# A fused recommender tower on one core: a split wait, a new cycle order and one more looked-up group

## The reference

```python
e = jnp.stack([tbl_0[ids[:, 0]], ..., tbl_39[ids[:, 39]]], axis=1)      # 2048 x 40 x 32
vi = e[:, _I_IDX, :]; vj = e[:, _J_IDX, :]                               # 780 pairs
z = jnp.einsum('bke,kef,bkf->bk', vi, W, vj)
h = jnp.concatenate([z, dense_ctx], axis=1)                              # 796 columns
h = jnp.maximum(h @ W_top1 + b_top1, 0.0)                                # 512
h = jnp.maximum(h @ W_top2 + b_top2, 0.0)                                # 256
y = h @ W_top3                                                           # 1
```

## Time and profile before

| | before |
|---|---|
| median of three runs | 696.76 us |
| profiled execution: time, span | 699.06 us, 697.2 us |
| TensorE matmul busy | 644.0 us (92%), 4800 records |
| VectorE busy | 580.5 us (83%), 578 instructions |
| ScalarE busy | 70.1 us (10%) |
| GpSimd busy | 460.5 us (66%) |
| L543 multiply, 440 instructions | 495.1 us |
| L567 transform | 242.4 us busy, 33.4 us idle ahead of it |
| L589 reduce | 217.7 us busy |
| L616 look-up | 65.2 us + 7.6 us busy |
| L493 units, 88 | 67.4 us |

### The profile page before, as it was taken

The page is one execution under the profiler, slowest core; times in us unless marked ns, Lnnn a source line. Parts: engine busy times, 40 slices in busy tenths (PEclk is TensorE's granted clock), DMA queues, the critical chain, the costliest instruction groups (busy, mean ns, idle before and its releaser), DMA issues.

```text
span 697.2 us, 11003 instructions
## 1 busy us (share of the span) xinstructions
PE 644.0 (92%) x4800; PEld 187.3 (27%) x4800; DVE 580.5 (83%) x578; ACT 70.1 (10%) x87; POOL 460.5 (66%) x471
## 2 busy tenths in 40 slices
PE   3898988988999999999999999998999999999898
PEld 1232222222223322322222222222222222222143
DVE  6988999999978799889877889889888888888800
ACT  5502001000100100110000000100000000000002
POOL 6777777777777777777777777777777777500000
PEclk9999999999999999999999999999999999999999
DMA  8735202000000110200000200000101000000000
GB/s 322 276 98 194 69 13 74 14 13 14 13 14 15 32 58 13 74 14 13 15 13 15 76 14 14 13 14 14 16 14 15 14 14 13 12 1 1 1 0 1
DMA packets 18944, 28.28 MB, mean 41 GB/s; under 512 B 8448, under 2 KB 16016, under 8 KB 17232
## 3 DMA queue, kind: packets, MB, share of 16 engines
q0 software_dynamic: 14848, 7.63, 7.4%
q1 hardware_dynamic: 3296, 17.57, 6.5%
q10 hardware_dynamic: 752, 2.37, 0.9%
HBM read 27.53 MB, written 0.01 MB: 40 GB/s over the span
## 4 chain that ended last, share of the span: by engine, by line
PE 61%; DVE 34%; issue 3%; DMA 1%; ACT 1%; ACTq 0%; SPq 0%; DVEq 0%
DVE prods L543 26%; PE tps L567 25%; PE zps L589 15%; PE mlp_ps L636 15%; DVE hot L493 6%; PE tps L636 4%; PE mlp_ps L616 2%; DMA ids<-in_hot_ids 1%; DVE eT L500 1%; PE zps L576 1%; DVE parts L482 0%; DVE zs L482 0%; ACTq L467 0%; ACT ids L409 0%; DVE w1s L482 0%
## 5 line engine op out<-in xcount | busy, mean ns | idle before, releaser
L543 DVE TENSOR_TENSOR prods<-tps,eT 128x1024 f32<-128x1024 f32 (+1 forms) x440 | 495.1, 1168 | 72.5 <-PE tps L567 68.8
L371 POOL DMA_INDIRECT rows<-in_table,idx x464 | 459.9, 991 | 144.4 <-issue 141.2
L567 PE MATMUL tps<-eT,weights 32*128 32x512 f32 x1680 | 242.4, 641 | 33.4 <-DVE prods L543 31.1
L589 PE MATMUL zps<-prods,select 128*32 128x512 f32 x1680 | 217.7, 605 | 2.3 <-DVE prods L543 1.5
L567 PEld LDWEIGHTS tps<-eT,weights 32*128 32x128 f32 x1680 | 66.7, 183 | 185.3 <-DVE prods L543 146.4
L636 PE MATMUL mlp_ps<-zs,w1s 128*128 128x512 f32 x182 | 89.8, 615 | 0.0
L589 PEld LDWEIGHTS zps<-prods,select 128*32 128x32 f32 x1680 | 38.2, 108 | 159.4 <-DVE prods L543 98.7
L616 PE MATMUL mlp_ps<-hot,parts 128*32 128x512 bf16 x960 | 65.2, 389 | 14.7 <-DVE hot L493 10.9
L493 DVE TENSOR_SCALAR hot<-ids,code 128x2048 bf16<-128x2048 int16 (+1 forms) x88 | 67.4, 787 | 1.9 <-ACT ids L409 1.6
L387 ACT ACTIVATE zs<-zps 128x512 f32<-128x512 f32 x28 | 16.7, 598 | 326.3 <-PE zps L589 326.3
L636 PEld LDWEIGHTS mlp_ps<-zs,w1s 128*128 128x128 f32 x182 | 31.3, 189 | 55.1 <-issue 55.1
(11 more groups left out here) (31 smaller groups left out, 50.4 us busy)
## 6 DMA issues: line engine op xcount, KB each, us to landing
ids<-in_hot_ids SPq DMA_DIRECT2D x10, 1024.0 KB
rows<-in_table,idx POOLq DMA_INDIRECT x464, 2.4
zs<-in_hot_table SPq DMA_DIRECT2D x4, 512.0 KB, 7.5
w1s<-in_w ACTq DMA_DIRECT2D x1, 1792.0 KB, 7.6
weights<-in_wt SPq DMA_DIRECT2D x1, 1088.0 KB
zs<-in_hot_ids SPq DMA_DIRECT2D x1, 1024.0 KB
weights<-in_wt SPq DMA_DIRECT2D x1, 960.0 KB, 9.1
weights<-in_wt SPq DMA_DIRECT2D x1, 704.0 KB, 7.2
```

What stands on the lines that cost most here:

```text
L371: pool.indirect_dma_start(rows[:, k % ROW_SLOTS, m * EMB:(m + 1) * EMB], None, table, bass.IndirectOffsetOnAxis(ap=idx[:, g, t, m:m + 1], ...
L543: last = dve.tensor_tensor(prods[:, at % PROD_SLOTS, r:to + 1, :], tps[:, pair, r % 2:to % 2 + 1, :], eT[:, (t * GROUPS + c) % ET_SLOTS, : ...
L567: last = pe.matmul(tps[:, (2 * at + half) % PAIR_BANKS, r % 2, :], weights[part, n, :], eT[part, slot, :], start=True, stop=True)
L589: last = pe.matmul(zps[EMB * r:EMB * (r + 1), :], select[:, off:off + EMB], prods[:, at % PROD_SLOTS, r, :], start=kt < KT - 1 and n == fi ...
```

## The change

The changed kernel has the following edits.

- Transform waits ahead of each half, for 2 * at - 2 and for 2 * at - 1.
- Cycles are listed in CYCLES: quad 0 of each chunk is a cycle of one quad, and then come 26 cycles of two, all from an odd n. The `between` order is gone. A cycle with one step now has the order T, R, M, T, R; a cycle with two or more keeps T, M, M, T, R, R.
- HOT_COUNT is (4, 4, 2, 2): group 3 of chunk 1 is looked up, not gathered. It comes first of chunk 1's hot groups, since its table stands in w1s. ET_SLOTS goes from 13 to 14. The 32 units of chunk 1 are spread over chunk 0 as the 24 were, and the loads of the perceptron's weights come after the drain of the new group.
- Units are made 4 quads ahead in every chunk (in the earliest cycles, from quad 4 on, where that is less). The conversions of ids move with them.
- In chunk 3, the 17 batches stand in its first 17 cycles of two. Six steps of the tail, those of the first output tile of layer one for k = 0 to 5, stand alone in cycles n = 37, 39, 41, 43, 45 and 51, and leave the tail.
- ScalarE writes a small tile minus_code and VectorE a tile ones. ScalarE's own way of making units is there, but `by_scalar` is always false: nothing reads these two tiles.

```diff
-ROW_SLOTS, ET_SLOTS, PROD_SLOTS = 6, 13, 3
+ROW_SLOTS, ET_SLOTS, PROD_SLOTS = 6, 14, 3
-HOT_COUNT = (4, 3, 2, 2)
-HOTS = [(t, g) for t in range(CHUNKS) for g in range(HOT_COUNT[t])]
+HOT_COUNT = (4, 4, 2, 2)
+HOTS = [(t, g) for t in range(CHUNKS) for g in ((3, 0, 1, 2) if t == 1 else range(HOT_COUNT[t]))]
+CYCLES = [at for t in range(CHUNKS) for at in [(t * QUADS,)] + [(t * QUADS + n, t * QUADS + n + 1) for n in range(1, QUADS, 2)]]
...
-        for k, block in enumerate(blocks):
-            at = cycles[k if hots else k * len(cycles) // len(blocks)]
+        for at, block in zip(twos, blocks):
...
+    for k, n in enumerate(EARLY_AT):
+        sides[(CHUNKS - 1) * QUADS + n].append(("mlp", CHUNKS - 1, 0, 0, k))
...
+EARLY_AT = (37, 39, 41, 43, 45, 51)
+EARLY = [("mlp", CHUNKS - 1, 0, 0, k) for k in range(len(EARLY_AT))]
+def by_scalar(h, u):
+    return False
-MADE_AHEAD = (2, 4, 4, 4)
+MADE_AHEAD = 4
-            MAKES[side_at - MADE_AHEAD[side_at // QUADS]].append(item[1:])
+            MAKES[max(side_at - MADE_AHEAD, min(side_at, 4))].append(item[1:])
-    return steps, int(len(steps) > 0 and at % QUADS % PER_KT == 0)
...
+            act.wait_ge(code_built, 1)
+            act.activation(minus_code[:, :], code[:, :], ACT.Copy, scale=-1.0).then_inc(codes_turned, 1)
...
-                        if step[0] == HOT_COUNT[0] - 1:
+                        if HOTS[step[0]] == (1, HOT_GROUPS - 1):
...
-                wait(pe, multiplied, 2 * at - 1)
                 for half in range(2):
+                    wait(pe, multiplied, 2 * at + half - PAIR_BANKS + 1)
                     for r in (2 * half, 2 * half + 1):
...
-            for at in range(0, TOTAL, 2):
-                steps, between = steps_of(at)
+            for cycle in CYCLES:
+                at = cycle[0]
+                steps = steps_of(at)
...
+                together = len(steps) > 1
                 transform(at)
-                for _, t, layer, m, k in steps[:len(steps) - between]:
+                if not together and at > 0:
+                    reduce(at - 1)
+                for _, t, layer, m, k in steps:
                     mlp(t, between_banks, layer, m, k)
-                if not steps and at > 0:
-                    reduce(at - 1)
                 look_ups(at)
-                transform(at + 1)
-                if steps:
-                    reduce(at - 1)
-                for _, t, layer, m, k in steps[len(steps) - between:]:
-                    mlp(t, between_banks, layer, m, k)
-                reduce(at)
-                look_ups(at + 1)
+                if len(cycle) == 2:
+                    transform(at + 1)
+                if together:
+                    reduce(at - 1)
+                if len(cycle) == 2:
+                    reduce(at)
+                    look_ups(at + 1)
...
-                        mlp(CHUNKS - 1, last_banks, layer, m, k)
+                        if ("mlp", CHUNKS - 1, layer, m, k) not in EARLY:
+                            mlp(CHUNKS - 1, last_banks, layer, m, k)
```

More of the change, by code:

```diff
@@ L143, in plan_sides @@
         hots = [h for h, (t_, _) in enumerate(HOTS) if t_ == t + 1]
-        cycles = [at for at in range(0, TOTAL, 2) if t * QUADS <= at < (t + 1) * QUADS]
+        twos = [cycle[0] for cycle in CYCLES if len(cycle) == 2 and cycle[0] // QUADS == t]
         first = 3 * M1
@@ L170 @@
         if item[0] == "hot" and item[1] >= HOT_COUNT[0]:
[L171 removed]
+            MAKES[max(side_at - MADE_AHEAD, min(side_at, 4))].append(item[1:])
 def steps_of(at):
[L177 to L178 removed]
+    return [item for item in SIDES[at] if item[0] == "mlp"]
 def use_of(item):
@@ L189 @@
 FIRST_MADE = {unit[0]: at for at, made in MAKES.items() for unit in made if unit[1] == 0}
-SHORTENED_AT = {max(at // 2 * 2 - 4, 4): h for h, at in FIRST_MADE.items() if h >= HOT_COUNT[0]}
-assert len(SHORTENED_AT) == len(HOTS) - HOT_COUNT[0]
+SHORTENED_AT = {max(at - (at % QUADS + 1) % 2 - 4, 3): h for h, at in FIRST_MADE.items() if h >= HOT_COUNT[0]}
+assert len(SHORTENED_AT) == len(HOTS) - HOT_COUNT[0] and set(SHORTENED_AT) <= {cycle[0] for cycle in CYCLES}
 def wait(engine, semaphore, count):
@@ L199, in hots_until @@
 def hots_until(t, g):
-    return sum(h <= (t, g) for h in HOTS)
+    return HOTS.index((t, g)) + 1
 def gathered_until(t, g):
@@ L243, in build @@
         code = sb("code", [PART, UNITS], I32)
+        minus_code = sb("minus_code", [PART, UNITS])
+        ones = sb("ones", [PART, 1])
         hot = sb("hot", [PART, HOT_SLOTS, Q, CHUNK], BF16)
@@ L342, in _ @@
             sp.wait_ge(ids_short, 1)
[L343 removed]
+            sp.wait_ge(hot_made_dve, 2)
             load_ids(2)
@@ L417, in round_part, with make_unit @@
                 act.activation(part_of[g][part], raw_parts[g], ACT.Copy).then_inc(rounded, 1)
+            def make_unit(h, u):
+                if u == [by_scalar(h, u_) for u_ in range(UNITS)].index(True):
+                    act.wait_ge(ids_short, h + 1)
+                act.wait_ge(hot_used, h * UNITS + u - HOT_SLOTS + 1)
+                columns = hot[:, (h * UNITS + u) % HOT_SLOTS].rearrange("p q c -> p (q c)")
+                act.activation(columns, ids16[:, h % 2].rearrange("p q c -> p (q c)"), ACT.Abs,
+                               bias=minus_code[:, u:u + 1]).then_inc(distances, 1)
+                act.wait_ge(distances, made_until(h, u, True))
+                act.activation(columns, columns, ACT.Relu, scale=-1.0, bias=ones[:, 0:1]).then_inc(hot_made_act, 1)
             def drain_hot(h):
@@ L447, in _ @@
             round_part(3, 1)
+            act.wait_ge(code_built, 1)
+            act.activation(minus_code[:, :], code[:, :], ACT.Copy, scale=-1.0).then_inc(codes_turned, 1)
+            act.wait_ge(codes_turned, 1)
+            act.wait_ge(consts_built, 2 + Q)
             shorten(3)
-            for at in range(0, TOTAL, 2):
+            for cycle in CYCLES:
+                at = cycle[0]
                 if at in SHORTENED_AT:
                     shorten(SHORTENED_AT[at])
-                if at == QUADS // 2 * 2:
+                if at == QUADS:
                     act.wait_ge(mlp_loaded, 16 * 5)
-                steps, between = steps_of(at)
-                if not between:
-                    drain_tiles(steps)
+                drain_tiles(steps_of(at))
                 drain_sums(at - 1)
-                if between:
-                    drain_tiles(steps)
-                drain_sums(at)
-                for kind, *step in SIDES[at] + SIDES[at + 1]:
+                if len(cycle) == 2:
+                    drain_sums(at)
+                for kind, *step in [item for quad in cycle for item in SIDES[quad]]:
                     if kind == "hot" and step[1] == UNITS - 1:
                         drain_hot(step[0])
-                        if step[0] == HOT_COUNT[0] - 1:
+                        if HOTS[step[0]] == (1, HOT_GROUPS - 1):
                             for dst, src in ((w1s, w1), (w2s, w2), (w3s, w3), (b1s, b1), (b2s, b2)):
                                 act.dma_start(dst[:], src).then_inc(mlp_loaded, 16)
+                for unit in [unit for quad in cycle for unit in MAKES[quad]]:
+                    if by_scalar(*unit):
+                        make_unit(*unit)
             drain_z(CHUNKS - 1, KT - 1)
@@ L489, in make_unit @@
                     dve.wait_ge(code_built, 1)
-                elif u == (2 if h == 0 else 0):
+                elif u == (2 if h == 0 else [by_scalar(h, u_) for u_ in range(UNITS)].index(False)):
                     dve.wait_ge(ids_short, h + 1)
@@ L511, in _ @@
                            1.0).then_inc(consts_built, 1)
+            dve.memset(ones[:, :], 1.0).then_inc(consts_built, 1)
             rest(0, 0)
@@ L549, in _ @@
                 for unit in MAKES[at]:
-                    make_unit(*unit)
+                    if not by_scalar(*unit):
+                        make_unit(*unit)
                 if at == 0:
```

28 lines of the change are left out of this document (18 added, 10 removed).

## The result

The changed kernel takes 694.12 us in the median of six runs (692.44 to 695.22), the kernel before 698.20 us in the median of its six (696.74 to 700.43). The ratio is 0.9936, with a 95% interval from 0.9920 to 0.9951: faster by 0.6%. The forecast was 690.2 us with a range of 685 to 698. All ratios leave out executions that took over 1.5% longer than the fastest of the same kernel.

The account below looks back on a forecast made before the run. VectorE bounds chunk 0, TensorE chunks 1, 2 and the tail, chunk 3 is mixed. Terms +1.5 - 0.4 - 4.7 + 2.2 - 5.2 = -6.6 us take 696.76 to 690.2 us, range 685 to 698.

Parts of the forecast that it names:

- the tail: After the last reduction, TensorE alone: six steps leave at 0.86 us each, -5.2 us.
- the cycle order of chunk 2: Chunk 2: five cycles with a step between two reductions take the plain order, saving 3.9 of the chunk's 4.7 us.
- the split wait: Transforms on TensorE: first half starts earlier, closing 16 VectorE gaps in chunk 0, -3.0 us; 0.37 per cycle without steps.
- the new group: Chunk 0: eight more units on VectorE cost +5.3 us, look-ups at the chunk's end +0.8; saved gathers give nothing.
- The conversion: Chunk 0, ScalarE: ids converted ahead of the last drain, so VectorE no longer waits 1.61 us, -1.6 us.
- Chunk 1: Second chunk: only the one cycle without work gains, -0.4 us.
- Chunk 3: Last chunk: early steps +3.2, two empty cycles -0.7, dense rows moved to an empty cycle -0.3; together +2.2 us.
- The last cycle: Last of six single-step cycles in the last chunk: the transform of quad 52 comes 0.4 us later.
- the loop of a lone step: Last chunk: cycles T R M T R take 5.47 us against 4.91, five times 0.56, 2.8 us more.
- that the split gives nothing: Rival: both halves' records leave together and gaps stay; sum -1.7, 695.1 us; 0.17 together with a dearer group in chunk 0.
- the slower case: Rival: a transform's second half queues behind the first, ready 0.39 us later in 49 loops, +19 us, 709 us; chance 0.08.
- The better case: Rival: less TensorE idle time at chunk 0's start, 1 to 3 us, and cheaper early steps, 2: 686 us; chance 0.13.

Follow-up runs that it names:

- e3b: Changed kernel with HOT_COUNT (4, 3, 2, 2) as before, so group 3 of chunk 1 is gathered, 29 gathered groups: 685.64 us, 0.9817 of the kernel before.
- e5: Changed kernel without split wait, new looked-up group and early steps, leaving cycle order, earlier units and earlier conversion: 692.25 us, 0.9919 of the kernel before.
- e1b: Changed kernel with the one wait of before ahead of each transform: 697.33 us, 0.9983 of the kernel before.
- e9: Kernel before with one number changed, so ScalarE converts the first ids of chunk 1 ahead of chunk 0's last drain: 695.34 us, 0.9967 of before.
- e4b: Changed kernel with EARLY_AT empty, all steps of the last chunk's perceptron in the tail: 693.37 us, 0.9926 of the kernel before.
- e2b: Kernel before with only the wait split by half: 690.12 us, 0.9885 of the kernel before.
- e1: Changed kernel with one wait per transform, first run, on a chip that stopped engines: 1.0007 of the kernel before (0.9963 to 1.0052).
- e4: Changed kernel with no early steps, first run, on a chip that stopped engines: 0.9954 of the kernel before (0.9912 to 0.9995).

## Why the prediction was right, and where it was off

The forecast said faster, by 6.6 us, mostly from the tail, the cycle order of chunk 2 and the split wait, with the new group as the price. All four have the sign that it gave, and the experiments bear it out: without the wait the kernel is slower, without the group it is faster. Leaving the early steps out made the kernel 0.6 us faster in the profiles: what the tail gained, chunk 3 paid. By its steps:

- **The split wait, chunk 0, -3.0.** Right in mechanism and near in size: 3.65 us for e3b against e5, both without the new group and at full clock. Beside the group's units it is only about 1.4 (e1b), because they fill places where gaps stood. A met wait costs nothing, as assumed: cycles with two steps still take 5.91 us.
- **The new group, +5.3 and +0.8.** Mis-sized. It is 7.2 us in the profiles. The units are 6.3, of which 1.0 is the slow ones, and ScalarE's order at quad 39 costs 0.9, a wait that the prediction did not look for. The 0.8 for the end of the chunk is there, but not from the group: the gap at quad 50 is 1.6 us in the changed kernel, and e3b without the group has 0.7 and 0.8 at quads 49 and 50. It goes with the 0.9 us that e5 is behind e9.
- **The conversion, -1.6.** Right: VectorE's wait is gone, and 1.65 us with it at full clock (e9).
- **Chunk 1, -0.4; chunk 2, -4.7.** Measured -0.6 and -3.9. The five odd cycles, read as 3.9 from the earlier trace rows, gave 3.6 (e5); but the split wait gave chunk 2 only 0.3, not 0.7. A cycle without steps fell from 5.06 to 4.58 us, and the two-step cycle behind a chunk's first quad rose from 5.90 to 6.11: part of what VectorE gains is only time for which TensorE would have waited later.
- **Chunk 3, +2.2.** Measured +3.3. Two steps failed in size. The last cycle was to grow by 0.4 us and grew by 1.05 (7.28 against 6.23 in e4b). And the loop of a lone step is 5.6 us and not 5.47, 0.7 over the five cycles. A reduction with a step behind it takes 617.48 - 616.48 = 1.00, and a lone step 618.53 - 617.48 = 1.05, where the prediction took halves of pairs, 0.92 and 0.96. The page TensorEngine Tiling (Array Packing) of the Trainium skill, Key Properties, says that a change of tiling mode drains TensorE. The trace fits that: a pair shares the price of going in and out, a lone block pays it alone, here 0.08 and 0.09 us more. That it is the drain which costs this, no run here shows.
- **The tail, -5.2.** Measured 5.15.

In the profiled executions the span fell by 6.1 us, from 697.2 to 691.1, close to the 6.6, and that closeness is luck. In the medians the time fell by 4.1. The step that failed here is the one that carried the sum over: that the difference is the same on the profiled execution and on the median. The profile of before had two stretches at half clock in chunk 0, and that of the changed kernel none. The two places in both, first before:

```profile
40.00:45.00 5.00, 5.00 (x60) 2.19 (x56) 5.00 (x8) 0.00 (x0) 3.78 (x5) 0.68 0.08 15
55.00:60.00 5.00, 3.54 (x20) 0.79 (x24) 4.93 (x6) 0.00 (x0) 4.02 (x4) 0.68 1.00 375
```

```profile
40.00:45.00 5.00, 5.00 (x74) 1.94 (x68) 5.00 (x9) 1.91 (x1) 3.98 (x4) 1.00 0.48 167
55.00:60.00 5.00, 5.00 (x54) 1.35 (x50) 5.00 (x6) 0.00 (x0) 3.78 (x5) 1.00 0.06 10
```

The six executions of the changed kernel show what such a stretch costs: spans of 690.6 and 691.1 us at a mean clock of 1.000, 692.3 and twice 692.4 at 0.998, 693.4 at 0.995. By the means of these three groups the first costs 1.5 us and the second 1.0. Its profiled execution was one of the two without any, and that of before had two; against the changed kernel's execution at the same 0.995 the difference is 697.2 - 693.4 = 3.8 us, 0.55%, which is what the ratio shows within its interval. At 1.000 and 0.998 it is 4.0 and 3.0 us, by later executions of the kernel before (694.8 and 695.4 us in the median). So the sum of the terms, 6.6, was some 3 us too large for two kernels at one clock. The terms give that too: chunk 0 came to +2.8 and not +1.5 (-3.65 for the wait, -1.65 for the conversion, +0.9 and +7.2), chunk 3 was 1.1 over and chunk 2 0.8 over, less 0.2 in chunk 1. The profile hid it with 2 to 3 us of clock, and the stated range held in spite of it. The remaining 1.4 us between 690.2 and 694.12 are the median of before itself, 696.76 in three runs and 698.20 in six.

The rivals: that the split gives nothing is refuted by e1b and e2b. That halves which start apart queue behind each other, the slower case, is refuted by the rows of e2b. The better case, a start of chunk 0 with less idle time and full clock, came true in part: e9 and the changed kernel have no half-clock stretch in chunk 0 in their profiles, and VectorE's gap ahead of quad 4 is 0.64 us and not 2.2. It is not shown that the edits took the stretches away: e1b has the earlier conversion too, and a stretch at 56 us, and four of the changed kernel's six executions have a clock below 1.000. Two of the signs that would have spoken for the forecast were missed as well: chunk 0 is not 1.5 us longer in the profile, and each chunk behind the first has a two-step cycle of 6.11 us.

## What to carry to other kernels

Before work is put on an engine, ask which stage it lands in: eight units cost 5 to 6 us in the one chunk where VectorE was the bound, to spare 16 gathers and a transpose that nothing waited for, and undoing this one edit was worth more than the whole change. Where a wait guards two buffers, a wait for each is free when it is met and takes a gap away when it is not; test it alone, since it gave 8 us by itself and 3.3 beside the other edits of this change, which filled some of its gaps with units and some with steps. And a step moved out of a tail is worth its price only if the loop that it enters doesn't run through it: the same six steps cost 0.6 us behind a reduction that waits and gained 1.9 ahead of it.

## What the runs showed of the hardware

Two of the four matmuls of a transform take as long alone as all four together: from their start to the reduction behind them it is 55.62 - 54.49 = 1.13 us (changed kernel), and 637.72 - 636.65 = 1.07 for all four (e2b). Started apart, the second two run beside the first: a transform of 1.52 us holds a wait of 0.4 and one full length, not two.

In the profiled execution of the kernel before, TensorE ran at half clock (1.2 GHz) for 3.4 us from 39.8 us and again from 56.8 us. Ahead of the first it had been idle for 1.3 us at 37 us, ahead of the second for 2.5 us at 54 us. In e9 one such stretch came in chunk 2, at 471 us, behind a wait of TensorE for VectorE:

```profile
469.43 1.14 PE L567 MATMUL tps<-eT,weights 32*128 32x512 f32 x8 [1.81 <-DVE prods L543]
470.50 1.76 PE L589 MATMUL zps<-prods,select 128*32 128x512 f32 x8
```

The reduction takes 1.76 us and not 1.06. In the changed kernel TensorE waited 1.00 us at 53.5 us, and no stretch followed. Why one wait brings a stretch and another doesn't is open. The number of stretches differs from one execution of the same kernel to another, so a profile's clock belongs beside its span whenever a difference of 0.5% is read from it.

On the chip of e1 to e4 the kernel before took 1.63 times as long (1136.78 us in the median), at a mean granted clock of 0.80 to 0.83. Where neither a stop nor half clock came between, TensorE's blocks took what they take elsewhere (1.07 us from a transform to the reductions behind it in e1, at 412.80). A line of e1's waits there (engine, line, releaser: us, times, longest us):

```profile
DVE prods L585 <- remote: 241.6, 49, 30.4
```

VectorE stood still up to 30 us at a time although what it waited for was done: the multiply at 450.9 us reads a transform that ended at 418.2. What did it is open, and so is whether the lower clock follows from the stops.
